# ScalarE issues its half of a stage 3 load four steps after the transpose that frees the buffer

## The reference

```python
# layer 1: adj is used as a matrix of eigenvectors
x_spec = einsum('nk,nc->kc', adj, x)
coefs  = exp(-evals * max(t, 1e-8))[:, None]
x      = layernorm(x + einsum('nk,kc->nc', adj, coefs * x_spec))
# layer 2: a graph convolution
adj_hat = adj + eye(N)
out     = (adj_hat / rowsum(adj_hat)) @ (x @ W) + b
x       = layernorm(x + tanh(out))
```

## The kernel before

| load | first step | buffer free after step | ACT issues before, at position |
|---|---|---|---|
| 32, 33, 34 | 134, 138, 142 | 121, 125, 129 | 121, 125, 129 |
| 35 | 146 | 137 | 137 |
| 38, 39, 40 | 160, 164, 168 | 141, 145, 149 | the same |
| 41, 42, 43 | 172, 176, 180 | 151, 155, 159 | the same |
| 44, 45, 46, 47 | 184, 188, 192, 196 | 163, 167, 171, 175 | the same |

## Time and profile before

### The profile page before, as it was taken

The page is one execution under the profiler, slowest core; times in us unless marked ns, Lnnn a source line. Parts: engine busy times, 40 slices in busy tenths (PEclk is TensorE's granted clock), DMA queues, the critical chain, the costliest instruction groups (busy, mean ns, idle before and its releaser), DMA issues.

```text
span 611.5 us, 8026 instructions
## 1 busy us (share of the span) xinstructions
PE 582.9 (95%) x2478; PEld 449.1 (73%) x2478; DVE 510.5 (83%) x572; ACT 399.0 (65%) x856; POOL 368.9 (60%) x215
## 2 busy tenths in 40 slices
PE   6999999999998998989999999999999989999993
PEld 5888888888876565758888888888888766666561
DVE  4899999999899998888899799595776677899992
ACT  5999999999996746455555655455444535555462
POOL 0000000000157987778999999778886898987882
PEclk9999999999999999999999999999999999999997
DMA  8999999999999999799969999198995399999101
GB/s 308 409 409 407 409 409 408 409 409 409 408 313 335 327 335 339 201 247 293 260 184 267 243 296 311 48 258 204 249 254 140 109 345 348 348 342 329 37 19 51
DMA packets 125065, 174.67 MB, mean 286 GB/s; under 512 B 6884, under 2 KB 105700, under 8 KB 125032
## 3 DMA queue, kind: packets, MB, share of 16 engines
q1 hardware_dynamic: 72608, 121.68, 59.2%
q10 hardware_dynamic: 52424, 52.58, 30.6%
HBM read 172.13 MB, written 2.11 MB: 285 GB/s over the span
## 4 chain that ended last, share of the span: by engine, by line
PE 76%; POOL 9%; DVE 8%; issue 3%; ACT 3%; ACTq 1%; DMA 1%; DVEq 0%
PE ps L836 13%; PE ps L838 12%; PE ps L837 12%; PE ps L808 9%; PE ps L809 9%; PE ps L810 9%; POOL lo L457 7%; PE ps L832 7%; DVE vt L665 4%; DVE lo L648 1%; PE ps L899 1%; PE ps L902 1%; ACTq L355 1%; ACT hi L512 1%; PE ps L793 1%
## 5 line engine op out<-in xcount | busy, mean ns | idle before, releaser
L457 POOL TENSOR_TENSOR lo<-vt,hi 128x1024 fp32r<-128x1024 f32 x126 | 319.1, 2557 | 40.8 <-ACT hi L512 40.2
L665 DVE STREAM_TRANSPOSE vt<-raw 128x1024 f32<-128x1024 f32 x184 | 221.8, 1225 | 63.3 <-PE ps L838 51.8
L512 ACT ACTIVATE hi<-vt 128x1024 fp32r<-128x1024 f32 x159 | 165.7, 1060 | 124.7 <-DVE vt L665 109.3
L648 DVE TENSOR_TENSOR lo<-raw,hi 128x1024 fp32r<-128x1024 f32 x124 | 157.9, 1278 | 16.5 <-ACT hi L498 8.4
L498 ACT ACTIVATE hi<-raw 128x512 fp32r<-128x512 f32 x256 | 158.8, 622 | 5.3 <-DMA raw<-in_adj_dram 1.8
L423 POOL TENSOR_TENSOR lo<-raw,hi 128x1024 fp32r<-128x1024 f32 x4 | 10.2, 2558 | 169.3 <-ACT hi L498 169.3
L808 PE MATMUL ps<-hi,xg_hi 128*128 128x512 f32 x256 | 100.3, 392 | 1.5 <-DVE lo L648 1.4
L810 PE MATMUL ps<-hi,xg_lo 128*128 128x512 f32 x256 | 99.7, 390 | 0.0
L809 PE MATMUL ps<-lo,xg_hi 128*128 128x512 f32 x256 | 99.7, 390 | 0.0
L836 PE MATMUL ps<-hi,s_hi 128*128 128x512 f32 x224 | 95.0, 424 | 4.9 <-POOL lo L457 4.3
L836 PE MATMUL ps<-hi,p_hi 128*128 128x512 f32 x206 | 88.8, 431 | 4.6 <-POOL lo L457 4.6
(11 more groups left out here) (71 smaller groups left out, 535.3 us busy)
## 6 DMA issues: line engine op xcount, KB each, us to landing
raw<-in_adj_dram SPq DMA_DIRECT2D x63, 1024.0 KB, 15.9
raw<-in_adj_dram SPq DMA_DIRECT2D x90, 512.0 KB, 10.1
raw<-in_adj_dram ACTq DMA_DIRECT2D x88, 512.0 KB, 12.0
late_raw<-in_adj_dram SPq DMA_DIRECT2D x8, 512.0 KB, 12.5
late_raw<-in_adj_dram ACTq DMA_DIRECT2D x8, 512.0 KB, 14.0
xn<-in_x_dram SPq DMA_DIRECT2D x8, 256.0 KB, 15.5
x_sb<-in_x_dram SPq DMA_DIRECT2D x8, 256.0 KB, 13.9
out_dram<-x_sb ACTq DMA_DIRECT2D x7, 256.0 KB, 2.9
```

Of the source, the lines that this page charges most:

```text
L457: nc.gpsimd.tensor_tensor(lo[:, slot(p), :], vt[:, slot(p), :], hi[:, slot(p), :].bitcast(f32), ALU.subtract).then_inc(pool_lo_ready, 1)
L512: nc.scalar.activation(hi[:, slot(s), :], vt[:, slot(s), :], ACT.Copy).then_inc(hi_ready, 1)
L648: nc.vector.tensor_tensor(lo[:, q % RING1, :], raw[:, k, 2 * h:2 * h + 2, :].rearrange("p r n -> p (r n)"), hi[:, q % RING1, :].bitcast(f3 ...
L665: nc.vector.transpose(vt[:, slot(s), :].rearrange("p (m a i) -> p m a i", m=2, a=RB), load_buffer(st.load).rearrange("p (a m e i) -> p e m ...
```

## The change

In `more_loads`, ACT issues its two quarters of a load at the position of the step that freed the buffer. With the change, this holds for positions of stage 2 alone; at the positions of stage 3 it issues them four positions later (`DEFER = 4`). It stands after `hi_step` of that position, as before. Eleven loads are concerned: 35 moves from position 137 to 141, 38 to 40 from 141, 145, 149 to 145, 149, 153, and 41 to 47 likewise from 151 to 155 and so on, up to 179. The loads 32 to 34 and 36, 37 stay. No DMA is added or taken out, SP's quarters stay as they are, and the wait of DVE for all four quarters stays.

```diff
+    DEFER = 4
...
             def more_loads(s):
 
-                n = STEP[s].load
-                if s == LAST_STEP[n] and n in BEFORE:
-                    load_quarters(act, BEFORE.index(n), (2, 3))
+                for n in range(NL):
+                    if BEFORE[n] is not None and s == LAST_STEP[BEFORE[n]] + (DEFER if STEP[s].visit == NG else 0):
+                        assert DEFER == 0 or LAST_STEP[BEFORE[n]] > END2[LAST] or STEP[s].visit < NG
+                        load_quarters(act, n, (2, 3))
```

## The result

| | before | after |
|---|---|---|
| median, us | 616.44 (10 runs, 612.41 to 619.55) | 621.42 (10 runs, 619.61 to 624.01) |
| span of the profiled execution, us | 611.5 | 619.4 |

The ratio is 1.0086, with a 95% interval of 1.0063 to 1.0109: slower by nine tenths of a per cent, which is 5.3 us by the ratio, while the two medians lie 5.0 us apart. The two profiled executions are 7.9 us apart, since the one before lies at the low end of its runs and the one after in the middle of its own. Up to step 141 they agree, except that the changed one is some 0.3 us later from its start on; every other difference of TensorE's times arises behind that step.

A forecast was written before the change was run, and what follows sets the result against it. TensorE, busy 95% of the time, was taken to bound the kernel. Load 35's lateness cost +2.0 us, of which 1.53 us of idle time took back all but 0.5; 619.18 + 0.5 = 619.7 us, range 616 to 625.

The forecast's parts named there:

- TensorE's idle time bounds the gain: From 478 to 600 us TensorE idles 4.55 us; with clock loss 6.3 us, 1.0% of the time.
- Loads 38 to 47 cost nothing: Issued four steps, 6.7 us, later with 13 us or more to spare, so still 6 us left.
- a sign of error: The forecast would be wrong if the DMA engines ran dry and the later loads came late.
- Load 35 becomes third on ScalarE's queue, a half taking 6.03 us there: ACT's half of load 35 passes loads 36 and 37; queue order 36, 37, 35, at 6.03 us each.
- It is complete at 506.1: Landing of load 35: three halves from 488 us at 6.03 us each, bounds 505.3 and 511.3.
- after 508: Load 35 landing later than 508 us would show the forecast wrong.
- TensorE loses 1.7 us at L899: Four L577 end at 509.5, not 506.6, while L899 wants them at 507.8: 1.7 us idle.
- clock only: Rival: landing as forecast, but the idle at 508 lowers TensorE's clock, costing 1.8 us; +2.3, 621.5 us; chance 0.12.
- stalled pipe: Rival: load 35 takes fourth place, lands at 511.3, TensorE idles near 7 us; +7.5 us, 626.7; chance 0.12.
- Some 1.5 us are given back at step 159: TensorE's lateness of 2.0 us falls into its 1.53 us idle time before 533.78, leaving 0.5 us.
- From there the rest only shifts: After about 534 us TensorE is busy without a break, so everything later shifts by +0.5 us.
- ScalarE's issues become short, by a microsecond or less: ACT's issues after 495 us mostly under 1 us; gain between 0 and 0.97 + 1.18 us, already in the sum.

The follow-up runs named there:

- e2_not35: Kernel before, with ScalarE's issues of loads 38 to 47 four positions later and load 35 issued as before; 615.47 us, ratio 0.9976.
- e4_fill: Changed kernel plus sixteen small zero matmuls on TensorE in its idle time before L902; 620.66 us, ratio 1.0069 to the kernel before.
- e6: Kernel before, with VectorE's `lo` of step 160 made to wait for GpSimd's `lo` of step 159; median 617.8 us, ratio 1.0018.
- e11_not35_fill: e2_not35 plus nine small zero matmuls on TensorE before its wait for step 142; 614.73 us, ratio 0.9959 to the kernel before.

## Why the prediction held in its range and was wrong in its sum

The time, 621.4, lies in the range of 616 to 625, and "within 1%, load 35 is the exception" held. But the sum said +0.5 us where the medians say +5.0 and the ratio +5.3. That the time came within 1.7 us of the forecast 619.7 is luck: the 619.18 us that the sum was added to is the median of three runs and lay 2.7 us above the 616.4 of ten, which hid as much of the error. Its steps:

- *TensorE's idle time bounds the gain.* Right: no version that only moves issues gained more than 0.24% by its ratio.
- *Loads 38 to 47 cost nothing.* Right (e2_not35). The DMA engines did run half empty at 512 to 516 us, which I had named as a sign of error, and no load but 35 came late for it.
- *Load 35 becomes third on ScalarE's queue, a half taking 6.03 us there.* Right, and shown by moving it one place: 6.1 us between landings, and it lands 5.5 to 6.2 us sooner from the second place.
- ***It is complete at 506.1.*** This term of the sum failed: 509.0, or 508.6 on the scale of the profile before. The three times 6.03 us were counted from 488 as the bytes flow, and of the 3.4 us that an issue takes beside its bytes I had put 2 before the bytes and none behind. The first half on the queue landed 10.2 us after its second issue, at 496.8, where my count gave 494.0: 2.8 of the 2.9 us of error are in this first half. The two rows of the DMA queue in the section on the result show where. By 489 us the queue had moved 16 packets, so the bytes began some 0.9 us later than I took; by 495 it had moved 1002 of the half's 1024, so the landing came some 1.7 us behind the last byte. The mark that I had set for being wrong, "after 508", was passed.
- *TensorE loses 1.7 us at L899.* It idled 4.12 us, 2.4 us more, as load 35 landed 2.5 us later than forecast, and then lost 1.6 us by the lower clock (e4_fill). The second was my rival "clock only", and it does not need the "stalled pipe", whose condition (fourth place, landing at 511.3) was not met. At step 146 TensorE was 6.0 us behind, where I had 1.7.
- *Some 1.5 us are given back at step 159.* Right: from 5.9 us at step 158 to 4.3 us at 159. GpSimd's idle time before steps 152 and 156 did not both vanish, 1.66 us are left before 156, as ScalarE still issued load 41 there for 2.6 us.
- *From there the rest only shifts.* Wrong: 4.3 us at step 159 became 7.5 at 166 in the profiled executions. I had read "TensorE is busy without a break" as a reserve of VectorE and GpSimd behind it. In fact two `lo` 0.07 us apart in the profile before had fallen in the better order, and with the change they fell in the other, and the chain went over to VectorE. Compared with e6, which has the same order as the change, 4.3 us stand, near the 5.0 of the medians.
- *ScalarE's issues become short, by a microsecond or less.* Half right: those of loads 37, 39, 40, 43 and 44 did. Load 35's own took 1.64 and 2.85 us, and one each of loads 38, 41 and 42 took 2.2 to 2.4. No issue stood on the chain any longer at 500 to 556 us. Yet taking the two that stood there before off it brought 0.24% at most (e2_not35).

## What to carry to other kernels

Before moving a transfer later, ask which other transfers of the same queue it will then stand behind. Load 35's half, issued just behind that of load 37, landed 5.5 us later than when issued just ahead of it, nearly a whole half's 6 us, while two more positions of delay ahead of load 37 cost nothing measurable. And an in-order engine spreads a late load: the transpose that waited held ScalarE's copy for another group, and that held TensorE. Where an estimate of a landing decides, count it from a landing in the trace, not from when bytes may start.

## What the runs showed of the hardware

- ScalarE's issues of 512 KB each go quickly (0.32 to 0.92 us at 481 to 491 us in the kernel before and the changed one) while fewer than four of them are outstanding on its queue; those that followed with about four or more outstanding, up to 498 us, took 1.6 to 2.9 us, up to a quarter's own time of 3.0. The fourth of a row was issued in 0.66 us, the fifth in 1.64 and the sixth in 2.85 in the changed kernel.
- With sixteen small matmuls in the 4.1 us that TensorE otherwise idled, its clock behind them was 1.00 and not 0.59 (e4_fill); with nine in the 2.4 us before step 142 it was 1.00 and not 0.79 (e11_not35_fill).
- GpSimd's and VectorE's subtractions with two operands from on-chip memory did not run side by side at steps 159 and 160: whichever began second was longer by about what was left of the other, 2.92 us against 1.2 and 3.37 us against 2.4.
